# A vision tower with expert layer on one core: earlier queries and gather, constant products at the end, last quarter in two parts

## The chip, the core and the metric

One core of a Trainium2 chip runs the kernel. The metric is the device time of one execution in microseconds (us), the median of several runs. Engines: TensorE (PE; its weight loads are listed apart as PEld), VectorE (DVE), ScalarE (ACT), GpSimd (POOL) and SyncE (SP). Here POOL mostly issues indirect DMAs, and SP issues the plain ones.

## The reference

16 images of 128x512 become 1024 tokens of 64 numbers each. Everything is float32.

```
h = patches(x) @ W.T + b + pos                       # 8x8 patches
h = h + attention(layernorm(h))                      # 8 heads of 8; K softmax over tokens, Q softmax over channels,
                                                     # context = K V^T, out = Wr (context^T Q) + br, + its own input
z = layernorm(h)
p = softmax(z @ gate_w + gate_b); two best experts of 16, weights normed to sum 1
h = h + sum over the two: weight * ((silu(z @ w1[e]) * (z @ w2[e])) @ w3[e])
```

## The kernel before, in words

**Pairs and steps.** Images are taken two at a time, 8 pairs `m` = 0 to 7. All five engines have a program of their own, written out over one common count of steps `s` (the loops `for s in range(SPAN)`). A step is no barrier: it only fixes the order of an engine's instructions, and semaphores do the rest. Each pair has a plan, a tuple that gives for each of its attention and routing stages a time `k` within the pair; `step_of(m, k)` turns it into a step, mostly `BEGUN[m] + k`. Whole numbers, halves and three quarters are places in the step. On TensorE a step holds, in order: the expert layer's first product of group `g = s - 23` (`project_in`), `turn_hidden(g-1)`, the stages with whole `k` of the pairs under way (lower `m` first), `turn(g+2)`, `project_out(g-2)`, the stages at `k+0.5`, those at `k+0.75`, the turned gates, and the sums. VectorE and ScalarE have whole and half places only.

**Attention of a pair.** Embedding into `wide_ps` (L1407, L1413), its norm on DVE, a trip of the normed embedding through DRAM (`xi_scratch`, `hx`), keys (L1534) and their softmax, queries and values in four quarters `r` (`queries`, L1424 and L1427: one matmul of 512 columns for the biases and two of 256 columns; then DVE L1065 and L1068 take the maximum of each head and subtract it, ACT L784 copies the values), the exponential of the queries (ACT L787), the head sums (DVE L1035), context (PE L1460), scales (DVE L1074 to L1080), the mix (L1454), the turned queries (PE L1465, ACT L790), and the attention output (PE L1475, L1476). Quarters 0 and 2 share one half of `wide_ps`, 1 and 3 the other. Then the second norm, the gate's logits (L1481) and the choice of experts, `pick` (DVE L1135 to L1166, a chain of small operations), the rank of each token in its expert (PE L1545 to L1548, waiting for `hot_sum` of `pick`) and its place (`find_places`, DVE L1212 to L1255).

**Expert layer.** POOL scatters the normed rows of a pair to DRAM, sorted by expert (L682, 32 indirect DMAs of 128 rows: 16 columns x 2 experts); TensorE works through 98 groups of four tiles (12 a pair, 13 for pairs 6 and 7): turned rows (L1612), two matmuls per tile against the expert's first weights (L1634), turned hidden (L1650), second weights (L1658); each result `y` is stored to DRAM by SP (L486). POOL then gathers each pair's results with 32 indirect DMAs (L699), ACT weighs them (`weigh`, L873) and DVE adds (`sum_up`, L1343, L1347). `GATHER[m]` is the step at which pair `m`'s gather stands in POOL's program, `SUMS[m]` those of its sums. A gather first waits until the pair's `y` is all stored, and POOL's step waits for `turn` of group `s - 23 + 1`. Pair 6 and 7 are scattered in pieces of three rows (L669).

**The last pair.** Pair 7 is gathered in pieces, 16 indirect DMAs `gather_pieces` (L711), one for each of 16 columns (8 blocks of tokens x 2 images), right behind pair 6's gather in POOL's program. TensorE sums them with the gated routes (`sum_pieces`, L1602): three products of 96 rows by 128 by 64 columns per column of tokens, which the profile counts as two records each, so 24 records in a quarter of four columns. Each quarter waits for its four gathers, then DVE adds `h2` (`sum_up_pieces`, L1333), and SP stores two DMAs (`store_result`, L493). The last quarter stands at step 128. The quarters lie in `turn_ps`, `hidT_ps` and the two halves of `h_ps`.

**Products of constants.** `keep_on` (L1431 to L1434) multiplies the identity by `pos_in` (512 columns) into `turn_ps`, whose result nobody reads; it stands once in the program, six products in pair 2's step 4. The profile counts two records a product.

Of the kernel before, what the change touches and what calls it, by code (L numbers as in the profile page):

```python
# [15 lines left out]
P = 128  # L16
IMAGES, MELS, FRAMES = 16, 128, 512
PATCH = 8
E = 64
# [5 lines left out]
PAIRS = IMAGES // 2  # L25
# [46 lines left out]
AT_ONCE = FIRST._replace(zturn=12, logits=12.5, pick=12.5, rank=13, count=13, odds=14.5, base=13.5, ends=13.5, owner=14)  # L72
PLANS = (AT_ONCE._replace(mean=3.5), AT_ONCE._replace(mean=2.5, mixed=8.5), FIRST._replace(embed=(0.75, 0.75, 1.75, 2)),
         LATER, LATER, LATER, LATER._replace(rank=15.5, count=15.5, base=16, tiles=16, bases2=16.75, moves=17, ends=17.5, owner=18),
# [20 lines left out]
SUMS = ([[43 + 14 * m + q for q in range(4)] for m in range(4)]  # L95
        + [[94, 95, 96, 97], [107, 108, 109, 110], [122, 123, 123, 124], [125, 126, 127, 128]])
STORED = 2
QUARTERS = 4
WARM = 6

ALONG = {4: ("att_ps_ready", 6), 8: ("k_ps_ready", 3), 12: ("logits_ps_ready", 2)}
# [48 lines left out]
def vit_kernel(nc, x, tok_w, tok_b, pos, wk, bk, wq, bq, wv, bv, wr, br, gate_w, gate_b, w1, w2, w3, out):  # L150
# [4 lines left out]
    with ExitStack() as ctx:  # L155
# [210 lines left out]
        y_stored = [sem(f"y_stored{n}") for n in range(2)]  # L366
        gathered = [[sem(f"gathered{n}_{q}") for q in range(QUARTERS)] for n in range(2)]
        rows_zeroed = [sem(f"rows_zeroed{n}") for n in range(3)]
        block = ctx.enter_context(nc.Block())
# [12 lines left out]
        def sums_at(s):  # L382

            for m in range(PAIRS):
                for q in range(QUARTERS):
                    if s == SUMS[m][q]:
                        yield m, q
# [46 lines left out]

        def quarter_place(q):

            return (turn_ps[:, 0:COLS * E // QUARTERS], hidT_ps[:, 0:COLS * E // QUARTERS],
                    h_ps[:, 0:COLS * E // QUARTERS], h_ps[:, 512:512 + COLS * E // QUARTERS])[q]

# [5 lines left out]
        def _(sp):  # L445
# [42 lines left out]
            def store_result(m, q):  # L488
                wait(sp, "result_ready", QUARTERS * m + q + 1)
                for b in range(2):  # L490
                    t0 = q * BLOCKS // QUARTERS
                    dst = out[2 * m + b, t0 * P:(t0 + BLOCKS // QUARTERS) * P, :].rearrange("(t s) e -> s t e", s=P)
                    sp.dma_start(dst, result[apart(m)][:, t0:t0 + BLOCKS // QUARTERS, b, :]).then_inc(result_out[apart(m)], 16)  # L493

# [50 lines left out]
            for n, pairs in enumerate((PAIRS - 1, 1)):  # L545
                sp.wait_ge(result_out[n], 16 * 2 * QUARTERS * pairs)
            for n in range(3):
# [3 lines left out]
        def _(pool):  # L551
# [150 lines left out]
            def gather_pieces(m, j):  # L702

                q = j // (COLS // QUARTERS)
                if j == 0:
                    for n in range(2):
# [4 lines left out]
                gp.indirect_dma_start(y_pieces[j][0:PIECES, :], None, y_dram[m % 3].rearrange("(c i) e -> c (i e)", i=PIECE),  # L711
                                      bass.IndirectOffsetOnAxis(ap=piece_from[0:PIECES, j:j + 1], axis=0)).then_inc(gathered[0][q], 16)

# [197 lines left out]
        def _(dve):  # L911
# [416 lines left out]
            def sum_up_pieces(m, q):  # L1328
                blocks = slice(q * BLOCKS // QUARTERS, (q + 1) * BLOCKS // QUARTERS)
# [3 lines left out]
                ve.tensor_tensor(result[0][:, blocks], quarter_place(q).rearrange("p (t b e) -> p t b e", b=2, e=E), h2[m % RING][:, blocks],  # L1333
                                 ALU.add).then_inc(S["result_ready"], 1)
# [44 lines left out]
        def _(pe):  # L1379
# [50 lines left out]

            def keep_on():  # L1431

                for n in range(WARM):
                    te.matmul(turn_ps[:, :], ident[:, :], pos_in[:, :, :].rearrange("p t e -> p (t e)"), start=True, stop=True)  # L1434

            def attend(m, k):

                plan, wide_ps, side_ps = PLANS[m], wides[second(m)], sides[second(m)]
                if (m, k) == (2, X_NEXT):
                    keep_on()  # L1440
                for quarter in range(4):
# [149 lines left out]
            def sum_pieces(m, q):  # L1591

                if q == 0:
                    wait(pe, "gates_turned", COLS)
                    wait(pe, "rowsT_ready", GROUPS_ALL)
                    wait(pe, "hidT_ready", GROUPS_ALL)
                    wait(pe, "hid_done", 2 * GROUPS_ALL)
                wait_on(pe, gathered[0][q], 16 * 2 * COLS // QUARTERS * (gathers(m) - 1) + 16 * COLS // QUARTERS)
                for i in range(COLS // QUARTERS):
                    j = q * COLS // QUARTERS + i  # L1600
                    for n in range(PIECE):
                        mm = te.matmul(quarter_place(q)[:, i * E:(i + 1) * E], pieces[1][j][0:PIECES, n * P:(n + 1) * P],  # L1602
                                       y_pieces[j][0:PIECES, n * E:(n + 1) * E], start=(n == 0), stop=(n == PIECE - 1))
                mm.then_inc(S["y_ps_summed"], 1)
# [108 lines left out]
```

## Time and profile before

| | |
|---|---|
| median of 3 runs | 737.89 us (735.17 to 743.90) |
| the profiled execution's own time | 742.13 us |
| its span, first to last instruction | 740.4 us |
| mean granted TensorE clock | 0.906 of full speed |
| PE busy | 84% of the span |
| POOL busy | 66% |
| DVE busy | 67% |
| ACT busy | 49% |

A row of the timeline gives start, duration, engine, line, operation, output<-input, how many instructions were merged, and in brackets the idle time before and what ended it. A row of the chain gives start, duration and what the chain went through. A row of the windows gives busy time (and number of instructions) of PE, PEld, DVE, ACT and POOL in a stretch, then the granted clock of TensorE (1.00 is 2.4 GHz, 0.50 is 1.2 GHz), the DMA engines' share and GB/s.

### The profile page before, as it was taken

The page shows a single profiled execution, that of the slowest core. Times are in us where ns is not written, and L with a number is a line of the kernel's source. Part 1 is how long each engine was busy: PE and PEld are TensorE (multiplying, and loading weights), DVE is VectorE, ACT ScalarE, POOL GpSimd, SP SyncE. Part 2 cuts the span into 40 slices and gives each one's busy share as a digit, 9 for nine tenths or more (in the row PEclk, how much of TensorE's full clock was granted, in tenths as well). Part 3 has the DMA queues.
Part 4 walks back from the last instruction along what each step waited for, and adds up shares of the span by engine and source line. Part 5 has one row for each costly group of instructions (what it writes and reads, how often), then busy time and mean ns, then how long its engine had stood idle before and what let it go on. Part 6 is the DMA issues. An engine that isn't in the chain of part 4 may idle for free.

```text
span 740.4 us, 14231 instructions
## 1 busy us (share of the span) xinstructions
PE 619.8 (84%) x4126; PEld 517.0 (70%) x4126; DVE 493.4 (67%) x1369; ACT 361.4 (49%) x795; POOL 488.2 (66%) x521
## 2 busy tenths in 40 slices
PE   5886687679799998999979998997878877987938
PEld 3465455577589867886868687966768767977938
DVE  5654675667546776777667756768578797776920
ACT  2121323045355646664666456643656556766730
POOL 5354047767575677777777777777747756777773
PEclk9958899699899999999999989998889999988955
DMA  3398604244274347544745284536435446655442
GB/s 83 82 182 325 241 30 128 70 123 115 69 213 126 84 102 205 138 109 95 194 123 140 68 200 120 134 83 147 109 104 123 121 118 181 158 124 120 100 95 57
DMA packets 169740, 95.11 MB, mean 128 GB/s; under 512 B 99682, under 2 KB 153746, under 8 KB 169668
## 3 DMA queue, kind: packets, MB, share of 16 engines
q1 hardware_dynamic: 153524, 67.96, 36.1%
q0 software_dynamic: 15360, 25.85, 13.1%
q8 instruction: 39, 0.64, 0.4%
q10 hardware_dynamic: 784, 0.39, 0.2%
q14 instruction: 33, 0.27, 0.1%
HBM read 45.61 MB, written 48.55 MB: 127 GB/s over the span
## 4 chain that ended last, share of the span: by engine, by line
PE 52%; DVE 24%; issue 9%; DMA 6%; ACT 6%; POOL 2%; ACTq 0%; DVEq 0%; POOLq 0%
PE h_ps L1634 7%; PE wide_ps L1407 7%; PE y_ps L1658 6%; PE hidT_ps L1650 4%; PE turn_ps L1612 3%; PE wide_ps L1427 3%; DVE twice_y L1324 3%; DMA hx<-xi_scratch 3%; PE wide_ps L1534 2%; ACT sums L873 2%; DMA xi_scratch<-xi 2%; PE wide_ps L1413 2%; PE wide_ps L1475 1%; POOL sums L699 1%; PE wide_ps L1476 1%
## 5 line engine op out<-in xcount | busy, mean ns | idle before, releaser
L682 POOL DMA_INDIRECT rows_scratch<-z_parts,place x192 | 191.5, 998 | 106.4 <-issue 55.8
L699 POOL DMA_INDIRECT sums<-y_scratch,place x192 | 187.0, 974 | 66.2 <-issue 56.4
L1634 PE MATMUL h_ps<-w_hi,rowsT 128*128 (+1 forms) x392 | 116.3, 324 | 14.2 <-DVE hid_all L1326 14.1
L1324 DVE SCALAR_TENSOR_TENSOR twice_y<-tanh,h_ps 128x256 f32<-128x256 f32 (+1 forms) x196 | 81.1, 414 | 35.4 <-ACT tanh L826 22.3
L1634 PE MATMUL h_ps<-w_lo,rowsT 128*128 (+1 forms) x392 | 104.7, 293 | 0.0
L1658 PE MATMUL y_ps<-w_sb,hidT_all 128*128 (+1 forms) x784 | 101.9, 275 | 1.2 <-ACT twice_y L841 1.2
L1658 PEld LDWEIGHTS y_ps<-w_sb,hidT_all 128*128 128x128 f32 (+1 forms) x784 | 98.9, 198 | 1.6 <-issue 1.6
L1634 PEld LDWEIGHTS h_ps<-w_hi,rowsT 128*128 128x128 f32 (+1 forms) x392 | 78.0, 199 | 23.8 <-issue 20.2
L826 ACT ACTIVATE tanh<-h_ps 128x256 f32<-128x256 f32 (+1 forms) x196 | 70.3, 386 | 46.1 <-PE h_ps L1634 41.7
L1326 DVE SCALAR_TENSOR_TENSOR hid_all<-twice_y,h_ps 128x256 f32<-128x256 f32 (+1 forms) x196 | 82.4, 420 | 6.7
L1634 PEld LDWEIGHTS h_ps<-w_lo,rowsT 128*128 128x128 f32 (+1 forms) x392 | 78.7, 201 | 0.4
L1612 PE MATMUL turn_ps<-ident,rows_all 128*128 128x128 f32 (+1 forms) x392 | 62.8, 285 | 12.4 <-ACT rowsT L815 11.0
L1650 PE MATMUL hidT_ps<-ident,hid_all 128*128 128x128 f32 (+1 forms) x392 | 65.6, 294 | 6.1 <-issue 3.6
L815 ACT ACTIVATE rowsT<-turn_ps 128x512 fp32r<-128x512 f32 (+1 forms) x98 | 57.9, 591 | 25.6 <-PE turn_ps L1612 25.3
L835 ACT ACTIVATE hidT_all<-hidT_ps 128x512 f32<-128x512 f32 (+1 forms) x98 | 59.1, 603 | 15.1 <-PE hidT_ps L1650 13.6
L1612 PEld LDWEIGHTS turn_ps<-ident,rows_all 128*128 128x128 f32 (+1 forms) x392 | 47.5, 147 | 25.9 <-issue 23.5
L1407 PE MATMUL wide_ps<-w_patch,x_cols 64*128 64x512 f32 x224 | 56.1, 632 | 3.2 <-DVE w_patch L930 3.2
L1650 PEld LDWEIGHTS hidT_ps<-ident,hid_all 128*128 128x128 f32 (+1 forms) x392 | 47.3, 151 | 11.7 <-issue 11.1
L841 ACT ACTIVATE twice_y<-y_ps 128x256 f32<-128x256 f32 (+1 forms) x98 | 37.4, 381 | 12.0 <-PE y_ps L1658 7.3
L1343 DVE SCALAR_TENSOR_TENSOR sums<-sums,gate 128x64 f32<-128x64 f32 x96 | 20.9, 279 | 27.4 <-ACT sums L873 27.3
L784 ACT ACTIVATE vals<-wide_ps 128x256 f32<-128x256 f32 x28 | 10.8, 384 | 57.8 <-DVE qs L1068 57.8
L873 ACT ACTIVATE sums<-sums,mean_all,gate 128x64 f32<-128x64 f32 x96 | 34.2, 430 | 9.0 <-DMA sums<-y_scratch,place 9.0
(369 smaller groups left out, 1141.7 us busy)
## 6 DMA issues: line engine op xcount, KB each, us to landing
rows_all<-rows_scratch SPq DMA_DIRECT2D x72, 256.0 KB
rows_scratch<-tanh SPq DMA_DIRECT2D x3, 3276.0 KB
y_scratch<-twice_y SPq DMA_DIRECT2D x72, 128.0 KB
rows_all<-rows_scratch SPq DMA_DIRECT2D x26, 252.0 KB
xi_scratch<-xi SPq DMA_DIRECT2D x16, 256.0 KB
hx<-xi_scratch SPq DMA_DIRECT2D x14, 256.0 KB
out<-sums SPq DMA_DIRECT2D x56, 64.0 KB
x_in<-in_x SPq DMA_DIRECT2D x26, 128.0 KB
```

The costliest lines, as they stand in the source:

```text
L682: gp.indirect_dma_start(rows_dram[n], bass.IndirectOffsetOnAxis(ap=place[m % RING][:, r, j:j + 1], axis=0), z_parts[m % 2][:, j // 2, j % ...
L699: gp.indirect_dma_start(y_of[r][apart(m)][:, j // 2, j % 2, :], None, y_dram[m % 3][0:GROUPS[m] * GROUP * width(m), :], bass.IndirectOffse ...
L815: sc.activation(rowsT[g % 2][:, 0:GROUP * w], turn_ps[:, 0:GROUP * w], ACT.Copy).then_inc(S["rowsT_ready"], 1)
L826: sc.activation(tanh[0:w, j, :], h_ps[0:w, :].rearrange("p (j n h) -> p j n h", j=GROUP, n=2)[:, j, 0, :], ACT.Tanh, scale=0.5).then_inc(S ...
L835: sc.activation(hidT[g % 2][:, 0:GROUP * w], hidT_ps[:, 0:GROUP * w], ACT.Copy).then_inc(S["hidT_ready"], 1)
L1324: ve.scalar_tensor_tensor(twice[0:w, j, :], tanh[0:w, j, :], 1.0, halves[:, j, 0, :], ALU.add, ALU.mult).then_inc(S["twice_done"], 1)
L1326: ve.scalar_tensor_tensor(hid[g % 2][0:w, j, :], twice[0:w, j, :], 0.5, halves[:, j, 1, :], ALU.mult, ALU.mult).then_inc(S["hid_done"], 1)
L1407: te.matmul(wide_ps[:, b * 512:(b + 1) * 512], x_cols[second(m)][half, j, :], w_patch[half, j, :, :].rearrange("p t e -> p (t e)"), start= ...
L1612: mm = te.transpose(turn_ps[:, j * w:(j + 1) * w], rows[g % 3][0:w, j, :, :].rearrange("p n e -> p (n e)"), ident[0:w, 0:w])
L1634: mm = te.matmul(h_ps[0:w, j * 256:(j + 1) * 256], rowsT[g % 2][:, j * w:(j + 1) * w], w12[:, bass.ds(experts[g][j], 1), :, :].rearrange(" ...
L1650: mm = te.transpose(hidT_ps[:, j * w:(j + 1) * w], hid[g % 2][0:w, j, :], ident[0:w, 0:w])
L1658: mm = te.matmul(y_ps[0:w, j * E:(j + 1) * E], hidT[g % 2][:, j * w:(j + 1) * w], w3_sb[:, bass.ds(e, 1), :].rearrange("h a d -> h (a d)") ...
```

## The change

Four edits:

- Pair 2's plan: the four quarters of the queries stand at k = 5.75, 6, 6.5, 7 in place of 6, 6.5, 7, 7.5, their values (DVE and ACT) at 5.5, 6, 6.5, 7 in place of 6.5, 6.5, 7.5, 7.5, and the stages from the exponential to the mix half a step sooner. `attend`, the attention output, keeps k = 10.
- Pair 0's gather stands at step 37 of POOL's program in place of 38.
- Ahead of the last pair's sums TensorE runs products of constants into `side_ps`: four before the first part, two before the second, two before the third, one before the fourth, none before the fifth. The first ones wait for pair 6's last gather, for the last copied `y` and for the last owners.
- The last quarter is two parts of two columns each, with a semaphore of its own for the last two gathers (`gathered_last`), a place in `y_ps` for the fifth part, an addition on DVE for each part and two stores for each part.

```
-PLANS = (..., FIRST._replace(embed=(0.75, 0.75, 1.75, 2)),
+PLANS = (..., FIRST._replace(embed=(0.75, 0.75, 1.75, 2), queries=(5.75, 6, 6.5, 7), values=(5.5, 6, 6.5, 7), qexp=7, qsum=7.5, context=7.5,
+                             scales=8, mix=8, qturn=8.5, mixed=9),
-GATHER = (38, 51, 65, 78, 86, 99, 110, 123)
+GATHER = (37, 51, 65, 78, 86, 99, 110, 123)
-        + [..., [122, 123, 123, 124], [125, 126, 127, 128]])
+        + [..., [122, 123, 123, 124], [125, 126, 127, 128, 128]])
+PARTS = (0, 4, 8, 12, 14, 16)
+LATE = (4, 2, 2, 1, 0)
+        def part_signal(j):
+            return gathered_last if j >= PARTS[4] else gathered[0][j // (COLS // QUARTERS)]
+        def part_place(q):
+            return (turn_ps, hidT_ps, h_ps[:, 0:512], h_ps[:, 512:1024], y_ps)[q][:, 0:len(part_cols(q)) * E]
-            def keep_on():
-                for n in range(WARM):
-                    te.matmul(turn_ps[:, :], ident[:, :], pos_in[...], start=True, stop=True)
+            def keep_on(place, count):
+                for n in range(count):
+                    te.matmul(place[:, :], ident[:, :], pos_in[...], start=True, stop=True)
             def sum_pieces(m, q):
                 if q == 0:
                     ...
+                    wait(pe, "y_ready", GROUPS_ALL)
+                    wait(pe, "owner_ready", PAIRS)
+                    wait_on(pe, gathered[1][QUARTERS - 1], 16 * 2 * COLS // QUARTERS)
-                wait_on(pe, gathered[0][q], 16 * 2 * COLS // QUARTERS * (gathers(m) - 1) + 16 * COLS // QUARTERS)
-                for i in range(COLS // QUARTERS):
+                keep_on(side_ps, LATE[q])
+                if q < QUARTERS:
+                    wait_on(pe, gathered[0][q], 16 * 2 * COLS // QUARTERS * (gathers(m) - 1) + 16 * len(part_cols(q)))
+                else:
+                    wait_on(pe, gathered_last, 16 * len(part_cols(q)))
+                for i, j in enumerate(part_cols(q)):
                     ...
```

`store_result` and `sum_up_pieces` take the blocks of a part for the last pair, and the last wait of SP counts the two further stores.

## Rows read from the trace of the kernel before

**Rows 1.** The page's first part: busy time, share of the span, instructions

```profile
PE 619.8 (84%) x4126; PEld 517.0 (70%) x4126; DVE 493.4 (67%) x1369; ACT 361.4 (49%) x795; POOL 488.2 (66%) x521
```

**Rows 2.** The chain that ended last, its last pieces

```profile
713.79 2.68 DMA sums<-y_scratch,piece_from
...
716.61 5.35 PE turn_ps L1602 x24
...
727.08 10.25 PE h_ps L1602 x48
```

**Rows 3.** Windows of the end: idle stretch and the sums

```profile
707.00:716.50 9.50, 0.00 (x0) 0.00 (x0) 4.05 (x16) 3.32 (x10) 7.06 (x9) 0.50 0.50 111
716.60:737.40 20.80, 20.71 (x96) 20.53 (x96) 1.31 (x4) 0.00 (x0) 9.75 (x11) 0.50 0.25 62
```

**Rows 4.** Timeline of the end, and second products at the full clock

```profile
692.82 0.99 PE L1658 MATMUL y_ps<-w_sb,hidT_all 128*126 x8
...
711.23 1.43 ACT L873 ACTIVATE xi<-hx,mean_all,gate 128x64 f32<-128x64 f32 x4 [2.34 <-DMA kexp<-y_scratch,place]
...
728.48 0.91 POOL L711 DMA_INDIRECT sums<-y_scratch,piece_from  x1 [0.30 <-issue]
...
737.36 0.42 DVE L1333 TENSOR_TENSOR sums<-h_ps,h 128x256 f32<-128x256 f32 x1 [4.70 <-PE h_ps L1602]
```

**Rows 5.** Products of constants (timeline), keys (chain), and windows with the granted clock

```profile
112.37 5.31 PE L1434 MATMUL turn_ps<-pos_in,ident 128*128 128x512 f32 x12
...
39.07 3.78 PE wide_ps L1534 x4
...
43.00:49.00 6.00, 4.89 (x24) 4.49 (x23) 5.55 (x17) 2.31 (x4) 0.00 (x0) 0.50 1.23 182
...
112.40:117.70 5.30, 5.28 (x14) 2.06 (x12) 3.94 (x15) 2.03 (x3) 3.82 (x4) 1.00 0.70 183
143.30:146.70 3.40, 3.36 (x8) 2.72 (x9) 1.86 (x7) 0.49 (x2) 2.71 (x3) 0.50 0.25 69
146.70:151.00 4.30, 2.91 (x22) 2.48 (x22) 2.17 (x5) 1.71 (x3) 3.17 (x4) 1.00 0.74 224
```

**Rows 6.** Pair 2's queries and what follows: one window, then the timeline

```profile
131.90:135.10 3.20, 0.00 (x0) 0.00 (x0) 2.99 (x9) 0.00 (x0) 2.59 (x3) 0.50 0.13 41
...
137.12 0.77 PE L1424 MATMUL wide_ps<-qv_bias,ones_r 128*128 128x512 f32 x1
...
137.69 1.91 PE L1427 MATMUL wide_ps<-proj_qv,hx 128*128 128x256 f32 x4
...
142.00 0.41 DVE L1065 TENSOR_REDUCE qmax<-wide_ps 128x32 f32<-128x256 f32 x1
...
144.21 0.17 DVE L1170 TENSOR_SCALAR odds_sum<-odds 128x16 f32<-128x16 f32 x1 [0.56 <-ACT odds L809]
...
148.38 0.38 ACT L784 ACTIVATE vals<-wide_ps 128x256 f32<-128x256 f32 x1 [1.20 <-DVE qs L1068]
...
149.74 1.22 DVE L1035 TENSOR_REDUCE qsum<-qs 128x128 f32<-128x1024 f32 x1 [1.40 <-ACT qs L787]
...
153.37 1.09 PE L1465 MATMUL wide_ps<-ident,qs 128*128 128x128 f32 x8 [1.63 <-DVE qs L1080]
```

**Rows 7.** POOL: windows of two long stretches, and the timeline where it waited

```profile
244.00:540.00 296.00, 225.89 (x231) 0.96 0.52 129
...
628.20:729.40 101.20, 77.12 (x80) 0.84 0.50 118
...
155.18 0.96 POOL L682 DMA_INDIRECT rows_scratch<-z_parts,place  x1 [3.51 <-PE turn_ps L1612]
...
237.93 0.36 SPq L486 DMA_DIRECT2D y_scratch<-twice_y  x1
...
243.79 0.99 POOL L699 DMA_INDIRECT sums<-y_scratch,place  x1 [8.02 <-PE turn_ps L1612]
...
544.78 0.91 POOL L669 DMA_INDIRECT rows_scratch<-w_patch,piece_at  x1 [4.33 <-ACT w_patch L855]
```

More of the change, by code:

```diff
@@ L72 @@
 AT_ONCE = FIRST._replace(zturn=12, logits=12.5, pick=12.5, rank=13, count=13, odds=14.5, base=13.5, ends=13.5, owner=14)
-PLANS = (AT_ONCE._replace(mean=3.5), AT_ONCE._replace(mean=2.5, mixed=8.5), FIRST._replace(embed=(0.75, 0.75, 1.75, 2)),
+PLANS = (AT_ONCE._replace(mean=3.5), AT_ONCE._replace(mean=2.5, mixed=8.5), FIRST._replace(embed=(0.75, 0.75, 1.75, 2), queries=(5.75, 6, 6.5, 7), values=(5.5, 6, 6.5, 7), qexp=7, qsum=7.5, context=7.5,
+                                                                                               scales=8, mix=8, qturn=8.5, mixed=9),
          LATER, LATER, LATER, LATER._replace(rank=15.5, count=15.5, base=16, tiles=16, bases2=16.75, moves=17, ends=17.5, owner=18),
@@ L367, in vit_kernel @@
         gathered = [[sem(f"gathered{n}_{q}") for q in range(QUARTERS)] for n in range(2)]
+        gathered_last = sem("gathered_last")
         rows_zeroed = [sem(f"rows_zeroed{n}") for n in range(3)]
@@ L384, in sums_at @@
             for m in range(PAIRS):
-                for q in range(QUARTERS):
+                for q in range(len(SUMS[m])):
                     if s == SUMS[m][q]:
@@ L433, in piece_place, with part_cols, part_blocks @@
             return (turn_ps, hidT_ps)[j % 2][:, :] if in_between(m) else wide_ps[:, j % 2 * 512:(j % 2 + 1) * 512]
-        def quarter_place(q):
-            return (turn_ps[:, 0:COLS * E // QUARTERS], hidT_ps[:, 0:COLS * E // QUARTERS],
-                    h_ps[:, 0:COLS * E // QUARTERS], h_ps[:, 512:512 + COLS * E // QUARTERS])[q]
+        def part_cols(q):
+            return range(PARTS[q], PARTS[q + 1])
+        def part_blocks(q):
+            return slice(PARTS[q] // 2, PARTS[q + 1] // 2)
+        def part_signal(j):
+            return gathered_last if j >= PARTS[4] else gathered[0][j // (COLS // QUARTERS)]
+        def part_place(q):
+            return (turn_ps, hidT_ps, h_ps[:, 0:512], h_ps[:, 512:1024], y_ps)[q][:, 0:len(part_cols(q)) * E]
         def x_half(m, b, par):
@@ L490, in store_result @@
                 for b in range(2):
-                    t0 = q * BLOCKS // QUARTERS
-                    dst = out[2 * m + b, t0 * P:(t0 + BLOCKS // QUARTERS) * P, :].rearrange("(t s) e -> s t e", s=P)
-                    sp.dma_start(dst, result[apart(m)][:, t0:t0 + BLOCKS // QUARTERS, b, :]).then_inc(result_out[apart(m)], 16)
+                    blocks = part_blocks(q) if m == PAIRS - 1 else slice(q * BLOCKS // QUARTERS, (q + 1) * BLOCKS // QUARTERS)
+                    dst = out[2 * m + b, blocks.start * P:blocks.stop * P, :].rearrange("(t s) e -> s t e", s=P)
+                    sp.dma_start(dst, result[apart(m)][:, blocks, b, :]).then_inc(result_out[apart(m)], 16)
             def clear_rows(n):
@@ L545, in _ @@
             for n, pairs in enumerate((PAIRS - 1, 1)):
-                sp.wait_ge(result_out[n], 16 * 2 * QUARTERS * pairs)
+                sp.wait_ge(result_out[n], 16 * 2 * (QUARTERS * pairs + (len(PARTS) - 1 - QUARTERS) * (1 - n)))
             for n in range(3):
@@ L1328, in sum_up_pieces @@
             def sum_up_pieces(m, q):
-                blocks = slice(q * BLOCKS // QUARTERS, (q + 1) * BLOCKS // QUARTERS)
+                blocks = part_blocks(q)
                 wait(dve, "y_ps_summed", q + 1)
@@ L1429, in queries @@
                 mm.then_inc(S["qv_ps_ready"], 1)
-            def keep_on():
-                for n in range(WARM):
-                    te.matmul(turn_ps[:, :], ident[:, :], pos_in[:, :, :].rearrange("p t e -> p (t e)"), start=True, stop=True)
+            def keep_on(place, count):
+                for n in range(count):
+                    te.matmul(place[:, :], ident[:, :], pos_in[:, :, :].rearrange("p t e -> p (t e)"), start=True, stop=True)
             def attend(m, k):
@@ L1439, in attend @@
                 if (m, k) == (2, X_NEXT):
-                    keep_on()
+                    keep_on(turn_ps, WARM)
                 for quarter in range(4):
@@ L1597, in sum_pieces @@
                     wait(pe, "hid_done", 2 * GROUPS_ALL)
-                wait_on(pe, gathered[0][q], 16 * 2 * COLS // QUARTERS * (gathers(m) - 1) + 16 * COLS // QUARTERS)
-                for i in range(COLS // QUARTERS):
-                    j = q * COLS // QUARTERS + i
+                    wait(pe, "y_ready", GROUPS_ALL)
[7 more added lines that the diff above has]
+                for i, j in enumerate(part_cols(q)):
                     for n in range(PIECE):
-                        mm = te.matmul(quarter_place(q)[:, i * E:(i + 1) * E], pieces[1][j][0:PIECES, n * P:(n + 1) * P],
+                        mm = te.matmul(part_place(q)[:, i * E:(i + 1) * E], pieces[1][j][0:PIECES, n * P:(n + 1) * P],
                                        y_pieces[j][0:PIECES, n * E:(n + 1) * E], start=(n == 0), stop=(n == PIECE - 1))
```

7 lines of the change are left out of this document (3 added, 4 removed).

## The prediction, made before the changed kernel was run

> **What bounds the kernel now.** I read the page's busy shares, then the chain that ended last, then windows of its end, then POOL's timeline. The shares name no single engine: PE is busy 84% of the span, DVE 67%, POOL 66% [rows 1]. But POOL's busy time leaves out 0.30 us between two indirect DMAs. From 244 to 540 it issued 231 in 296 us, 1.28 us each, and from 628.2 to 729.4 80 in 101.2 us, 1.265 us each [rows 7]: there it never stops. In between it waits for others, as 4.33 us for a piece that ACT had to copy [rows 7]. So the first 628 us go at the pace of TensorE with DVE and ACT; from there POOL's 80 gathers (two pairs of 32 and 16 pieces) set the time, whatever TensorE does, until the last lands.
>
> The end is a second matter. The chain ends with a gather that takes 2.68 us to land, then 24, 24 and 48 records of L1602, 20.7 us in one piece [rows 2]. TensorE stood idle from 707 to 716.5 with its clock at 0.50 (1.2 GHz), and the clock stayed at 0.50 through all 96 records of the sums, 20.71 us busy of 20.80 [rows 3]. A record takes 10.25 / 48 = 0.213 us, a quarter 5.12 us. POOL supplies a quarter in 4.90 us: from the fourth gather at 713.79 [rows 2] to the sixteenth at 728.48 [rows 4] are twelve of 1.224. So TensorE at half clock is just slower than the supply, falls behind a little in each quarter, and starts the last one late: the last gather starts at 728.48, lands 2.7 us later at 731.2, and the last addition comes at 737.36 [rows 4], 6.2 us behind.
>
> **The change part by part.**
>
> *Products and the fifth part.* At the full clock the nearest rows to the sums are the second products (the same loads, 64 columns streamed): 8 records in 0.99 us, 0.124 each with the tail of the last one in it [rows 4]; half of 0.213 is 0.107. I take 0.112. So a full quarter takes 24 x 0.112 = 2.7 us and a half one 12 x 0.112 = 1.34 us. A product of constants took 5.31 / 6 = 0.88 us at clock 1.00 [rows 5]; at 0.50 I take the keys, of the same 512 columns, two matmuls in 3.78 us, 1.89 us each [rows 5].
>
> The first four products may start when pair 6's last gather has landed, 711.2 by ACT's wait for it [rows 4]. All four at 0.50 would end at 718.8. If the clock comes back after 3.4 us of them, as it did in the queries [rows 5], 1.8 are done and the other 2.2 take 1.9 us: 716.5; some us later or sooner moves this end by half as much. I take 717. The first four gathers of pieces are in at 716.5 [rows 2], so the others at 721.4, 726.3, 728.7 and 731.2. With the clock back, TensorE does this: part 1 from about 717 to 719.7, two products to 721.5, part 2 (in at 721.4) to 724.2, two products to 726.0, part 3 (in at 726.3) to 729.0, one product to 729.9, part 4 (in at 728.7) to 731.2, part 5 (in at 731.2) to 732.6. Each product lies in time in which TensorE would wait for POOL; no gap is above 0.6 us. The addition starts at 732.7 in place of 737.36: 4.65 us gained. Its cost falls from 0.42 to some 0.25 us, while two more stores go through SP, about 0.4 us each beside the last gathers; I count these as nothing together (-0.2 to +0.8). The new waits of TensorE hold nobody up: behind them stand only the sums, which could not start before 716.5. The range of this term: if the clock comes back during the sums, 2 to 4.6 us gained; if it never does, a loss (the rival below). I take 4.65, because products of constants kept the clock at 1.00 over 5.3 us, and because after 3.4 us of queries at 0.50 (8 records, 256 and 512 columns) it was at 1.00 again [rows 5]; ours are up to 7.6 us of the longest kind.
>
> One row speaks against this: the keys, 3.78 us without a pause at 0.50, were followed by six more microseconds at 0.50 [rows 5]. Twice that length lies before the first part, and the pairs of products between the parts come on top.
>
> The sums' own row says that their kind of work does not raise the clock: 20.7 us busy, and 0.50 to the last [rows 3]. The Trainium skill (TensorE: Matmul & The Clock Gate, Part 1: The HAM clock gate) says that the throttle is the default and that sustained activity of the engine releases it. By that rule the sums of before would have freed themselves in the first quarter, and the products would only take up time. This trace does not agree, at 0.213 us per record from the first to the last.
>
> *Queries of pair 2.* TensorE stood idle from 131.9 to 135.1, waiting for pair 1's `pick` on DVE [rows 6]. Quarter 0 of the queries costs 2.48 us at half clock (137.12 to 139.60) [rows 6]; at k = 5.75 it is ahead of pair 1's rank and fits into that hole. Its DVE part follows `pick` at 135.2 and is done by 136.1. Then, with the durations of rows 6: rank to 137.1 as before, quarter 1 to 139.6, its DVE part to 140.6, pair 1's `find_places` behind it to 142.7 (0.6 later than before), quarters 2 and 3 on TensorE meanwhile (to 143.4), their DVE parts of 0.9 us each to 144.5, the last copy of values to 144.9. Before, it ended at 148.76: 3.85 gained. A part is given back: pair 1's odds stand on ACT behind the exponential of pair 2 now, and DVE must do its weights (the four operations from 144.21 on [rows 6], some 0.2 each) before the head sums. These start at 147.1 in place of 149.74 [rows 6], 2.6 gained. The scales follow, so the turned queries come at 150.8 in place of 153.37 [rows 6], and so do the attention output and group 0. POOL, which waited 3.51 us for `turn` of group 1 at 155.18 [rows 7], starts 2.6 sooner. Bounds: 0 if one of the waits stays where it is, 3.85 if the weights cost nothing. I take 2.6.
>
> From there to 628 us nothing waits for a fixed time: all orders are as before, so the shift is carried by every engine. That is the weak step, over 470 us.
>
> *Pair 0's gather.* It started at 243.79, released by `turn` at step 38 [rows 7]. At step 37 the wait is for the last `y`, issued at 237.93 [rows 7] and in about 2.2 us later: a start at 240.5 or so, 3.3 sooner. Since POOL runs without a pause from there to 540, it keeps these 3.3 us, and then they go into the wait of 4.33 us for a piece at 544.78 [rows 7]: it becomes some 7.6. Nothing on TensorE waits long for these gathers or scatters before. I take 0; bounds: -0.5 (traffic met at another time) to 3.3 (all of it kept).
>
> **Sum.** 742.13 - 4.65 - 2.6 - 0 = 734.9 for the profiled execution. It lies 4.24 above the median shown, 737.89; the same 7.25 off the median gives 730.6.
>
> **Rivals.**
> A. *The clock does not come back at the end.* Then every product costs 1.89 us on the path: 711.2 + 4 x 1.89 = 718.8, first part to 723.9, 3.78 more, 5.12, 3.78, 5.12, 1.89, and 5.12 for parts 4 and 5: 748.7 in place of 737.3, 11.4 lost, less 2.6 from the front: 746.7. For it: the keys and the sums at 0.50. Against it: the queries and the products before. It decides from the point where the clock is still 0.50 at the end of part 2. Slower.
> B. *The front's gain is used up on the way* (a hole in TensorE's program, as DVE's chains leave, simply gets longer). Then only the end counts: 737.89 - 4.65 = 733.2. For it: POOL's and TensorE's many waits between 540 and 628. Against it: nothing there depends on time that the change does not move too.
> C. *The lead of POOL counts too*, because rows or stores wait for its scatters somewhere: up to 3.3 more, 727.3. For it: POOL has no pause in 296 us. Against it: the wait at 544.78, where POOL is the one that waits.
> D. *The clock comes, and falls again in the sums*, whose kind of work did not raise it: then one or two parts run at 0.213 us a record and 2 to 4 us of the 4.65 are lost: 733.6.
>
> **How the numbers follow.** The forecast 0.50, A 0.07, B 0.19, C 0.10, D 0.10; 0.04 is left for what I don't see. A measurement of this kernel can tell about 1% from no change, here 7.4 us, and the forecast, 730.6, lies on that bound of 730.5. Faster by over 1%: half of the forecast's chance, all of C, and some of the rest: 0.42. Within 1%: the other half, B and D: 0.51. Slower by over 1%: A: 0.07. The range goes from C (727) to above B and D with the runs' own spread: 736.
>
> **What would show it.** Right: TensorE's windows from about 716 on at 1.00, sum records 0.112 us apart, 64 columns as before; gaps of TensorE below 1 us between parts; the last addition some 1.5 us behind the landing of the last gather, at about 730 in the trace's time; quarter 0 of pair 2's queries in the hole near 132; head sums near 147.1; POOL's wait before pair 1's second lot of scatters below 1 us; POOL's last saturated run starting at 625.6. Wrong: any 0.50 window in the sums; head sums later than 148.5; a saturated run that starts at 628 or later.

## The result, and the profile after

| | before | changed |
|---|---|---|
| median of 20 runs each, taken side by side | 741.14 us (734.80 to 746.66) | 735.29 us (732.09 to 739.82) |
| the profiled execution's own time | 742.13 us | 738.46 us |
| its span | 740.4 us | 736.7 us |

The ratio is 0.9938, with a 95% interval of 0.9919 to 0.9957: the changed kernel is 0.6% faster (the two medians alone divide to 0.9921, near the lower end of that interval). Six of the study's 268 executions are recorded as slow (more than 1.5% above the fastest of their kernel) and left out of the ratios and of the fit below. The ratio's gain is 0.4% of the time less than the forecast (730.6 / 737.89 = 0.990). The 737.89 it started from was a low draw of three runs; over 117 runs of the kernel before, in all comparisons of this study, the mean is 740.6. In the changed kernel's profile the full level of TensorE's clock reads 0.95 where it reads 1.00 in the one before (the half level reads 0.50 in both). Of TensorE's times at the full level only the wide products are longer for it; rows for this stand at the experiment with the gather's step taken back.

The page's busy line and the last pieces of its chain (columns as in [rows 1, 2]):

```profile
PE 627.2 (85%) x4144; PEld 513.3 (70%) x4144; DVE 493.0 (67%) x1370; ACT 361.4 (49%) x795; POOL 488.1 (66%) x521
```

```profile
706.35 2.54 DMA kexp<-y_scratch,place
709.03 6.65 PE side_ps L1450 x8
715.68 2.64 PE turn_ps L1624 x24
718.32 1.84 PE side_ps L1450 x4
720.16 2.65 PE hidT_ps L1624 x24
722.80 1.85 PE side_ps L1450 x4
724.66 2.64 PE h_ps L1624 x24
...
728.25 1.29 PE h_ps L1624 x12
729.54 1.36 PE y_ps L1624 x12
```

The busy shares are those of [rows 1]; only PE's rose, by 7.4 us. Products were added and sums shortened, but the traces of this study with the same number of PE records spread from 619.4 to 629.5 us, so no cause is read from these 7.4 us. The chain shows the end that I forecast: four products in 6.65 us, mostly at half clock, then every full part in 2.64 us, where the first took 5.35 and the last two together 10.25 before [rows 2]. Windows of the same stretch (columns as in [rows 3]):

```profile
709.10:715.60 6.50, 6.50 (x10) 2.70 (x10) 1.30 (x5) 1.25 (x4) 4.98 (x6) 0.54 0.37 89
715.70:731.10 15.40, 15.19 (x106) 12.50 (x105) 1.74 (x5) 0.00 (x0) 8.65 (x10) 0.95 0.32 80
```

Granted clock 0.54 during the products and the full level in all five parts, where [rows 3] had 0.50 throughout. The timeline has POOL's last gather and the last addition:

```profile
726.18 0.91 POOL L727 DMA_INDIRECT sums<-y_scratch,piece_from  x1 [0.30 <-issue]
...
730.93 0.29 DVE L1349 TENSOR_TENSOR sums<-y_ps,h 128x128 f32<-128x128 f32 x1 [1.06 <-PE y_ps L1624]
```

The last addition starts 4.75 us behind the last gather's start; before it was 737.36 - 728.48 = 8.88 [rows 4]. So 4.13 us were gained at the addition, and yet the span ends 736.7 - 726.18 = 10.5 us behind the last gather, where before it ended 11.9 behind: 1.4 us gained. What lies between stands in the instructions that the trace puts on the program's block itself (here L155 before and L160 after; the columns are engine, operation, count, duration in ns min/median/max, first and last start). Before:

```profile
L155 POOLq DRAIN  x1: 22113/22113/22113, 716.7 to 716.7; - x1
...
L155 SPq DRAIN  x1: 7/7/7, 740.2 to 740.2; - x1
```

After:

```profile
L160 POOLq EVENT_SEMAPHORE  x2: 17/17/17, 736.5 to 736.6; - x2
...
L160 POOLq DRAIN  x1: 22273/22273/22273, 714.2 to 714.2; - x1
...
L160 SPq DRAIN  x1: 7/7/7, 733.3 to 733.3; - x1
```

A DRAIN stands at the end of each engine's program, with only semaphore events behind it. POOL's is recorded from early on, while its gathers are still being worked off, so its start says little; what matters is its end, start plus duration: 716.7 + 22.1 = 738.8 before and 714.2 + 22.3 = 736.5 after. Both are 10.30 us behind the start of the last gather. SyncE, which waits for the last result stores, reached its own DRAIN at 740.2 before and at 733.3 after. Before, the stores ended the run and POOL's drain was through 1.4 us earlier; after, the stores are done at 733.3 and the run waits for POOL to 736.5. The chain does not show this: it follows work, and ended with TensorE's last part.

The front in the timeline of after, first TensorE and VectorE around pair 2's queries, then POOL:

```profile
129.39 0.77 PE L1440 MATMUL wide_ps<-qv_bias,ones_r 128*128 128x512 f32 x1
...
132.15 0.61 DVE L1181 TENSOR_REDUCE hot_sum<-hot_b 128x16 f32<-128x256 bf16 x1
...
132.82 0.21 PE L1561 MATMUL hidT_ps<-ones,hot_sum 128*16 128x1 f32 x2 [0.95 <-DVE hot_sum L1181]
...
144.72 0.17 DVE L1186 TENSOR_SCALAR odds_sum<-odds 128x16 f32<-128x16 f32 x1 [1.50 <-ACT odds L825]
...
145.43 1.20 DVE L1051 TENSOR_REDUCE qsum<-qs 128x128 f32<-128x1024 f32 x1
```

```profile
150.85 0.95 POOL L699 DMA_INDIRECT rows_scratch<-z_parts,place  x1 [1.07 <-PE turn_ps L1634]
...
238.00 0.99 POOL L716 DMA_INDIRECT sums<-y_scratch,place  x1 [6.58 <-DMA y_scratch<-twice_y]
...
542.13 0.91 POOL L686 DMA_INDIRECT rows_scratch<-w_patch,piece_at  x1 [4.66 <-ACT w_patch L871]
...
625.88 0.97 POOL L716 DMA_INDIRECT sums<-y_scratch,place  x1 [0.30 <-issue]
```

Quarter 0 lies in the hole, whose rest is 0.95 us where it was 3.2 [rows 6]. Odds and weights now stand ahead of the head sums, which start at 145.43, 4.3 us sooner than the 149.74 of [rows 6]; but 2.3 of these were there already at pair 1's `hot_sum` (132.15 against 134.46, from other stretches at half clock ahead of it), so the queries' own share is 2.0. POOL's wait at 155.18 of 3.51 [rows 7] is one of 1.07, pair 0's gather starts at 238.00, released by the stored `y` and no longer by `turn`, and the unbroken run of 80 starts at 625.88 for 628.20: 2.3 us sooner. That this is near the 2.6 forecast is luck: head sums that start 4.3 us sooner should have moved it by 4.3, and from `hot_sum` to the last gather both traces take 594.0 us.

### The profile page after: what moved, and what is told of

The parts are those of the page before. It is cut to its first block, busy times and chain, and to the rows that moved or that the text cites. A ratio compares the mean times of both kernels' runs of the same rounds, so it can differ in the third digit from the quotient of the medians.

```text
span 736.7 us, 14271 instructions
## 1 busy us (share of the span) xinstructions
PE 627.2 (85%) x4144; PEld 513.3 (70%) x4144; DVE 493.0 (67%) x1370; ACT 361.4 (49%) x795; POOL 488.1 (66%) x521
## 4 chain that ended last, share of the span: by engine, by line
PE 51%; DVE 24%; issue 9%; ACT 6%; POOL 5%; DMA 4%; ACTq 0%; DVEq 0%; POOLq 0%
PE wide_ps L1423 7%; PE h_ps L1656 7%; PE y_ps L1680 5%; PE hidT_ps L1672 3%; PE turn_ps L1634 3%; PE wide_ps L1443 3%; DVE twice_y L1340 2%; PE wide_ps L1550 2%; POOL sums L716 2%; ACT sums L889 2%; PE wide_ps L1429 2%; DMA hx<-xi_scratch 2%; PE side_ps L1450 2%; DMA xi_scratch<-xi 1%; PE wide_ps L1491 1%
## 5 line engine op out<-in xcount | busy, mean ns | idle before, releaser
L1656 PE MATMUL h_ps<-w_hi,rowsT 128*128 (+1 forms) x392 | 116.5, 325 | 14.1 <-DVE hid_all L1342 13.9
L1656 PEld LDWEIGHTS h_ps<-w_hi,rowsT 128*128 128x128 f32 (+1 forms) x392 | 78.5, 200 | 24.4 <-issue 20.7
L1672 PEld LDWEIGHTS hidT_ps<-ident,hid_all 128*128 128x128 f32 (+1 forms) x392 | 46.1, 148 | 11.1 <-issue 10.3
L1423 PEld LDWEIGHTS wide_ps<-w_patch,x_cols 64*128 64x128 f32 x224 | 21.2, 194 | 24.2 <-issue 19.7
```

What stands on the lines that cost most here:

```text
L1423: te.matmul(wide_ps[:, b * 512:(b + 1) * 512], x_cols[second(m)][half, j, :], w_patch[half, j, :, :].rearrange("p t e -> p (t e)"), start= ...
L1656: mm = te.matmul(h_ps[0:w, j * 256:(j + 1) * 256], rowsT[g % 2][:, j * w:(j + 1) * w], w12[:, bass.ds(experts[g][j], 1), :, :].rearrange(" ...
L1672: mm = te.transpose(hidT_ps[:, j * w:(j + 1) * w], hid[g % 2][0:w, j, :], ident[0:w, 0:w])
```

## The experiments

Two theories after the result. The drain theory (called D in the expectations below; it is not the prediction's rival D): the front's gain arrived, and at the end only 1.4 us counts, because POOL's drain, 10.3 us behind its last gather, takes over from the stores. Its rival (E, with the prediction's B): the end was gained in full as computed, and most of the front's 2.6 us was lost on the way. A third question is which of the two front edits carries the front. All ratios are against runs of the kernel before on the same chip.

**One group of edits each.** The plan of pair 2 and the gather's step, with the old end:

```
-PLANS = (..., FIRST._replace(embed=(0.75, 0.75, 1.75, 2)),
+PLANS = (..., FIRST._replace(embed=(0.75, 0.75, 1.75, 2), queries=(5.75, 6, 6.5, 7), ...),
-GATHER = (38, ...
+GATHER = (37, ...
```

> Only the first two edits (pair 2's plan, pair 0's gather at step 37); the end is as before. Theory D (the end is held by POOL's drain, which ends 10.3 us after the start of the last gather, so the products and parts gain only about 1.4 us and the front carries the rest): 3 to 4 us below before, ratio 0.995 to 0.996; POOL's last run without a pause starts 2 to 4 us sooner than 628.2. Rival E (the end's 4.6 us are all gained and the front's are used up on the way, as rival B of the prediction said): within 1 us of before, ratio 0.999 to 1.001.

Measured: 736.96 us, ratio 0.9948 (0.9920 to 0.9976). In its trace the last 80 gathers start at 621.15, 7.1 us sooner than before, where 2 to 4 were expected: single executions differ by more than the edits are worth.

The products and the fifth part, with the old plan and step:

```
+LATE = (4, 2, 2, 1, 0)
+PARTS = (0, 4, 8, 12, 14, 16)
```

> Only the products and the fifth part; the front is as before. Theory D: 1.4 us below before, ratio 0.998; in the trace the last addition about 4.7 us after the start of the last gather, SyncE through some 7.2 us after it, POOL's drain 10.3 us after it, and the span ends 0.2 us behind that. Rival E: 4 to 5 us below before, ratio 0.994, and the end follows the last addition by about 3 us.

Measured: 738.64 us, ratio 0.9987 (0.9957 to 1.0017). The front carries the larger part and the end at most 0.43%, where the prediction gave it 4.65 us (0.63%). The two ratios multiplied give 0.9935, within the changed kernel's interval. E falls: its 0.994 for the end alone and its 0.999 to 1.001 for the front alone both lie outside the intervals. The trace of this kernel adds a case that the prediction had as its own rival D, the clock falling again in the sums (TensorE's timeline):

```profile
722.91 1.55 PE L1623 MATMUL h_ps<-sums,w_patch 96*128 96x64 f32 x12 [0.21 <-DMA sums<-y_scratch,piece_from]
724.30 1.50 PE L1623 MATMUL h_ps<-sums,x_in 96*128 96x64 f32 x12
725.64 1.96 PE L1449 MATMUL side_ps<-pos_in,ident 128*128 128x512 f32 x2
727.39 2.66 PE L1623 MATMUL h_ps<-sums,x_cols 96*128 96x64 f32 x12
729.84 2.77 PE L1623 MATMUL y_ps<-sums,squares 96*128 96x64 f32 x12
```

The last product takes 1.96 us and both half parts 2.7 instead of 1.5; the last addition comes 7.4 us behind the last gather (732.65 - 725.24). The span ends 10.5 us behind it all the same, by the drain. What I priced at 2 to 4 us in rival D costs nothing here.

**No products.** The changed kernel with

```
-LATE = (4, 2, 2, 1, 0)
+LATE = (0, 0, 0, 0, 0)
```

> The changed kernel without any product of constants (a count of 0 for each part); parts, waits and front stay. Sums run at clock 0.50 to the end, 0.213 us a record, the last addition about 8.9 us after the last gather's start. Theory D: the store of the last part then ends after POOL's drain again, so 1.0 to 1.5 us above the changed kernel, ratio to before about 0.996. Rival E: 4 to 5 us above the changed kernel, ratio to before 0.999 to 1.000.

Measured: 736.19 us, ratio 0.9925 (0.9897 to 0.9953), not to be told from the changed kernel; the 0.996 that the drain theory gave lies just outside, and E's 0.999 to 1.000 far outside. In its trace the last addition is 8.8 us behind the last gather and the span ends 11.4 behind it, by the stores, 0.9 later than with products. So by the trace all products together are worth 0.9 us, not four; the ratio, with an interval of 0.56%, cannot show so little.

**The drain itself.** The changed kernel with a wait on POOL for the landing of the last two gathers, and a no-operation behind it:

```
+                if j == COLS - 1:
+                    pool.wait_ge(gathered_last, 32)
+                    gp.nop()
```

> The changed kernel, with one wait more on POOL behind the last gather: for the landing of the last two gathers, then a no-operation. It asks what POOL's drain waits for. If it is a cost of its own that starts when POOL's last instruction is through, its end moves by the landing, 2.5 us and more, to 12 to 13 us after the last gather's start. If it is work left from the indirect DMAs themselves, it ends 10.3 us after the last gather's start as before, and the time stays.

Measured: 735.96 us in its one run, span 734.2. POOL's last gather starts at 721.93 in the timeline, and the block's instructions read:

```profile
L160 POOLq EVENT_SEMAPHORE  x2: 17/17/17, 734.0 to 734.1; - x2
...
L160 POOLq DRAIN  x1: 9381/9381/9381, 724.6 to 724.6; - x1
```

Now the DRAIN starts only when the gathers have landed, and its own length shows: 9.38 us. It ends 724.6 + 9.4 = 734.0, 12.03 us behind the last gather instead of 10.30, and the span follows it. So the 9.4 us are a cost of their own that begins when POOL is through with its last instruction (10.30 less the 0.91 of the gather is 9.39), not the landing of a transfer: a drain that only waited for the landing would have been over at once. This rests on one execution, but on its trace and not on its time.

**The two front edits apart.** The plan alone, and the step alone:

```
-PLANS = (..., FIRST._replace(embed=(0.75, 0.75, 1.75, 2)),
+PLANS = (..., FIRST._replace(embed=(0.75, 0.75, 1.75, 2), queries=(5.75, 6, 6.5, 7), ...),
```

> The kernel before with the new plan of pair 2 alone; the gather stays at step 38 and the tail is the old one. If the front's gain is the queries' (my prediction's 2.6 us, carried to the end): POOL's last run of 80 starts about 2.6 us sooner and the median is about 2.6 us (0.35%) below the kernel before, ratio 0.9965, nearly all of what both front edits together gave (0.9948). If instead POOL's lead carried the gain: no measurable difference, ratio 1.000. The end stays 11.9 us behind the last gather's start, by SyncE's stores.

Measured: 738.79 us, ratio 0.9986 (0.9951 to 1.0022).

```
-GATHER = (38, ...
+GATHER = (37, ...
```

> The kernel before with pair 0's gather at step 37 alone. If, as predicted, POOL's lead is swallowed by its wait for ACT's copied piece near 544 us: the gather starts 3 to 4 us sooner (about 240), the wait near 544 grows by as much, ratio 1.000 (-0.07% to +0.1%). If the lead counts at the end (rival C): up to 3.3 us faster, ratio 0.9955 to 0.997, and the run of 80 starts sooner than 628.2 by as much.

Measured: 741.12 us, ratio 0.9983 (0.9945 to 1.0021). Neither can be told from no change alone, and each interval holds both expectations. The trace of the plan alone, of the fastest of its 12 executions, has the last 80 gathers at 619.19, 9 us sooner, far from the 2.6 expected and again more than the edit. POOL's timeline of the second shows the mechanism:

```profile
238.61 0.99 POOL L699 DMA_INDIRECT sums<-y_scratch,place  x1 [4.93 <-DMA y_scratch<-twice_y]
...
544.77 0.91 POOL L669 DMA_INDIRECT rows_scratch<-w_patch,piece_at  x1 [6.19 <-ACT w_patch L855]
...
628.18 0.97 POOL L699 DMA_INDIRECT sums<-y_scratch,place  x1 [0.30 <-issue]
```

The gather starts 5.2 us sooner than the 243.79 of [rows 7] (1.8 of that were there at `hot_sum`), the wait near 544 grows from 4.33 to 6.19, another of 2.19 us stands at 537.67 where before there was none of over 2 us, and the last run starts at 628.18 against 628.20. In this execution the lead is gone by then, as the prediction had it. So is the lead of the head sums, which start at 145.57 here, 4.2 us sooner than before. Over all traces the growth of the waits is clearer: POOL's pauses of over 0.4 us between 300 and 560 us sum to 8.2 us on average in the four traces with step 38 and to 11.8 in the ten with step 37.

**Undone one at a time.** With the intervals so wide, the same question from the other side, the changed kernel with one front edit taken back:

```
-GATHER = (37, ...
+GATHER = (38, ...
```

> The changed kernel with pair 0's gather back at step 38. By my prediction (worth 0): the same as the changed kernel, ratio to the kernel before 0.994. By a least-squares fit over all runs so far, in which the step is worth 1.2 us with an uncertainty of 0.6: ratio 0.9955. By rival C (3.3 us): 0.9985.

Measured: 737.84 us, ratio 0.9956 (0.9921 to 0.9990). The interval holds all three expectations, that of the prediction's C too. The chain of this trace, whose full level reads 1.00, has two products and a full part:

```profile
717.88 1.77 PE side_ps L1450 x4
719.65 2.63 PE hidT_ps L1624 x24
```

In the changed kernel's chain, at 0.95, they took 1.84 and 2.64 us: the products are 4% longer and the sums are not.

```
-PLANS = (..., FIRST._replace(embed=(0.75, 0.75, 1.75, 2), queries=(5.75, 6, 6.5, 7), ...),
+PLANS = (..., FIRST._replace(embed=(0.75, 0.75, 1.75, 2)),
```

> The changed kernel with the old plan of pair 2; gather at 37 and the new tail stay. If the queries carry 2.0 to 2.6 us: ratio to the kernel before 0.9965 to 0.9975 (738.3 to 738.9). If they carry nothing to the end (rival B): 0.994, as the changed kernel. The local step shows in the stretch from pair 1's pick to group 0: about 20 us with the old plan, 17 to 18 with the new.

Measured: 737.69 us, ratio 0.9993 (0.9965 to 1.0021). By this ratio, taking the plan back gives up nearly all of the gain; median by median (737.69 / 739.84 = 0.9971) it gives up about half, as in the fit below, and as the 0.9965 to 0.9975 expected. The 0.994 that the prediction's B would give lies outside the interval. In its trace the head sums start 13.65 us behind `hot_sum`, and the last addition 4.15 behind the last gather, with the clock at its full level throughout the parts.

One kernel's runs spread over 1%, so I put them into one least-squares fit: 262 runs of 14 kernels, a level for each of the four groups of comparisons, a yes or no for each edit (kernels that differ from the changed one in their products or POOL's last wait count as having the new end), and one for the three kernels at the end of this section.

| edit | forecast, us | fitted, us, with 95% interval |
|---|---|---|
| pair 2's plan | -2.6 | -2.1 +/- 0.9 |
| pair 0's gather at 37 | 0 | -1.05 +/- 0.93 |
| products and five parts | -4.65 | -1.1 +/- 1.0 |
| the three together | -7.25 | -4.2 +/- 0.9 |

**Products ahead of the first part alone.** The changed kernel with

```
-LATE = (4, 2, 2, 1, 0)
+LATE = (4, 0, 0, 0, 0)
```

> The changed kernel with the four products ahead of the first part alone, and none between the later parts. If they raise the clock by themselves: the first part's 24 records take 2.65 us. If the products between keep it up: a later part falls to 0.50 (5.1 us for a full part, 2.6 for a half), and the last addition comes up to 4 us later behind the last gather. Either way the end stays 10.5 us behind the last gather, by POOL's drain, and the ratio to the kernel before is that of the changed kernel, 0.994, since even a last addition 7.4 us behind the gather leaves SyncE before the drain's end. If the sums bound the end: 1 to 3 us slower than the changed kernel.

Measured: 737.33 us, ratio 0.9962 (0.9930 to 0.9994). Its TensorE timeline:

```profile
713.70 2.79 PE L1624 MATMUL turn_ps<-sums,w_patch 96*128 96x64 f32 x24
717.95 4.26 PE L1624 MATMUL hidT_ps<-sums,w_patch 96*128 96x64 f32 x24 [1.46 <-DMA sums<-y_scratch,piece_from]
722.79 2.82 PE L1624 MATMUL h_ps<-sums,w_patch 96*128 96x64 f32 x12 [0.57 <-DMA sums<-y_scratch,piece_from]
725.40 2.77 PE L1624 MATMUL h_ps<-sums,x_in 96*128 96x64 f32 x12
...
730.52 2.77 PE L1624 MATMUL y_ps<-sums,squares 96*128 96x64 f32 x12
```

Part 1 runs at the full clock, and in part 2, after 1.46 us of waiting, the clock falls and stays down: 2.8 us for twelve records from then on. So here the four products raise it and do not keep it up. That those between the parts do is borne out by six of the eight traces that have them; in the other two the clock fell all the same, but only in the last product. The last addition is 8.16 us behind the last gather, and the span ends 10.80 behind: here the stores (10.58) are barely behind the drain (10.30), where the expectation had the drain at the end. The median is 2 us above the changed kernel's, where the trace's own difference is 0.3; the intervals overlap, so it does not contradict.

**Looking for a better version.** If the end is POOL's unbroken run plus its drain, gathers must leave that run. Pair 5's gather one step sooner puts four of them among pair 7's scatters, where POOL has gaps:

```
-GATHER = (37, 51, 65, 78, 86, 99, ...
+GATHER = (37, 51, 65, 78, 86, 98, ...
```

> The changed kernel with pair 5's gather one step sooner in POOL's program (98 in place of 99). If from some 626 us on the time is that of POOL's unbroken run of gathers and of its drain 10.3 us behind the last one, then gathers that go into POOL's idle gaps of 0.5 to 4.3 us among pair 7's scatters shorten the run: some 2 to 4 fewer than 80 in the last unbroken run, last gather 2 us or so sooner, median about 2 us (0.27%) below the changed kernel, ratio to the kernel before about 0.991. If TensorE or the stores of the last group bound the end instead, nothing is gained (0.9938) or, where the earlier gathers wait for a store still under way, up to 1.5 us are lost.

Measured: 734.93 us, ratio 0.9927 (0.9888 to 0.9966), which holds the 0.991 expected and the changed kernel's 0.9938 alike.

Two steps sooner puts eight there:

```
-GATHER = (37, 51, 65, 78, 86, 99, ...
+GATHER = (37, 51, 65, 78, 86, 97, ...
```

> The changed kernel with pair 5's gather two steps sooner in POOL's program (97 in place of 99). One step moved four gathers ahead of the last scatters (last unbroken run 628.7 to the end, 76 gathers) and the time was 0.9927 of the kernel before, against 0.9938. If POOL's remaining gaps among pair 7's scatters (2.9, 1.2, 1.8, 0.5, 1.8 and 0.8 us) can take gathers, the second step brings a further 1 to 2 us: ratio 0.990 to 0.992. If those gathers must wait for the last y of pair 5 or push the scatters that TensorE's next groups wait for, the gain is gone: 0.994 or more.

Measured: 734.78 us, ratio 0.9917 (0.9886 to 0.9949). POOL's timeline of the second, among the scatters:

```profile
611.44 0.91 POOL L686 DMA_INDIRECT rows_scratch<-w_patch,piece_at  x1 [0.30 <-issue]
612.66 0.97 POOL L716 DMA_INDIRECT sums<-y_scratch,place  x1 [0.30 <-issue]
...
617.69 0.93 POOL L686 DMA_INDIRECT rows_scratch<-w_patch,piece_at  x1 [0.30 <-issue]
```

The gaps behind 611 are gone: POOL's pauses of over 0.4 us between 560 and 640 us sum to 6.3 us, against 9.6 to 11.0 in the eleven traces with this gather at 99. The ratio's interval holds the expected 0.990 to 0.992 and the changed kernel's 0.9938. The last has the gather at 98, and pair 1's odds and weights behind pair 2's head sums:

```
-         AT_ONCE._replace(mean=2.5, mixed=8.5)
+         AT_ONCE._replace(mean=2.5, mixed=8.5, odds=15.5)
```

> The changed kernel with pair 5's gather at 98 and pair 1's odds one step later (15.5), behind pair 2's head sums. The weights' four small operations on DVE, about 0.7 us, and the wait for ACT's odds leave the path between pair 2's exponential and its head sums: group 0 comes 0.7 to 1 us sooner against pick, and the time is 0.7 to 1 us below that of the kernel with gather at 98 alone, ratio 0.991 to 0.992. If something else then binds the head sums (the exponential itself, as at the old place), no difference: 0.9927.

Measured: 736.70 us, ratio 0.9960 (0.9929 to 0.9991). Locally it does what was expected: DVE's row before the head sums is no longer a weight but an idle stretch that waits for the exponential,

```profile
145.65 1.22 DVE L1051 TENSOR_REDUCE qsum<-qs 128x128 f32<-128x1024 f32 x1 [1.29 <-ACT qs L803]
```

11.05 us behind `hot_sum` (134.60) against 12.14 in the kernel with 98 alone. The total does not show it: both expected ratios, 0.991 to 0.992 and 0.9927, lie below the interval. The three together fit to -0.8 +/- 1.2 us against the changed kernel. With a term for each they fit to -1.4 +/- 1.9 (98), -2.1 +/- 1.8 (97) and +0.9 +/- 1.8 (odds later): 97 is the best candidate, but as the best of three and just off zero it isn't shown to beat the changed kernel.

## Why the prediction was right or wrong

*The size of the gain.* Forecast 7.25 us for the profiled execution; measured 742.13 - 738.46 = 3.67, and -4.2 +/- 0.9 over all runs. The direction was right; 735.29 us lies inside the range of 727 to 736, but nearly all of the missing part belongs to one term.

*The step that failed: "The addition starts at 732.7 in place of 737.36: 4.65 us gained."* The sentence takes the last addition for the end of the span. The addition did come that much sooner: 4.13 us at a full level that reads 0.95, and 4.7 in the trace of the kernel with the old plan (last addition 4.15 behind the last gather; 4.2 was forecast). But a second thing ends behind the last gather, POOL's drain at +10.30, and it was only 1.6 us below the end of before at +11.90. The term is capped there: 11.90 - 10.53 = 1.37 us, fitted 1.1. With the cap in place of 4.65 the forecast for the profiled execution would have been 742.13 - 1.37 - 2.6 = 738.2; it was 738.46. That this is so close is luck, since a single execution varies by more; what bears the cap out is the fit and the table. The DRAIN's row stood in the trace of before, outside the chain and the timeline of work. A table of the traces shows the rule (us behind the start of the last gather):

| trace | last addition | stores in (SyncE) | POOL's drain ends | span ends |
|---|---|---|---|---|
| before | 8.88 | 11.68 | 10.30 | 11.90 |
| plan and gather | 8.87 | 11.67 | 10.30 | 11.89 |
| no products | 8.79 | 11.21 | 10.30 | 11.43 |
| four products | 8.16 | 10.58 | 10.30 | 10.80 |
| end alone | 7.41 | 9.82 | 10.31 | 10.54 |
| changed | 4.75 | 7.17 | 10.30 | 10.53 |
| wait on POOL | 4.10 | 6.51 | 12.03 | 12.27 |

In each row the span ends 0.22 to 0.24 behind the later of the two middle columns. The seven other traces follow the same rule: 10.53 in the five with all products, 11.84 and 11.86 in the two with the old end, POOL's drain at 10.30 in all seven.

*The clock (forecast 0.50, A 0.07, D 0.10).* Right in every trace with products ahead of the first part: it came back before the first part and A never occurred. It fell again within the last product in two traces (the end alone, and gathers at 97) and stayed in the six others with all products, so the prediction's D is real, and costless under the drain. The Trainium skill (TensorE: Matmul & The Clock Gate, Part 1: The HAM clock gate) has sustained activity release the throttle. The runs bear out what the prediction held against it: the sums alone, 64 columns a record, never raised the clock in the kernel before [rows 3], and with four products they ran to the end at half clock once it had fallen; products of 512 columns raised it each time.

*The queries (-2.6).* Right in mechanism, a little large. In the traces with the old plan the head sums start 15.28, 13.67, 12.95 and 13.65 us behind pair 1's `hot_sum` (mean 13.9); in the nine with the new plan and the odds where they were 12.2 on average: 1.7 us. At the end 2.1 +/- 0.9. The step I called weak, that the shift is carried over 470 us, held on average, by the fit: from `hot_sum` to the last gather the four traces with the old plan take 594.0 us and the seven with the new one (pair 5's gather at 99) 590.8, 3.3 +/- 2.7 us less. No single trace shows it: between the traces of before and after this stretch is the same, and with the gather's step alone the head sums' lead of 4.2 us is gone at 628.

*Pair 0's gather (0).* The lead goes into POOL's waits, as I said: 3.6 us more of pauses between 300 and 560 us with step 37, for 3.3 computed, though not in one wait (in the changed kernel's trace the one near 542 is 4.66 us, and 6.22 with the step taken back). The fit gives -1.05 +/- 0.93, just off zero. Between nothing and 2 us is what I can say; the 3.3 us of C are excluded by the fit. Through what a microsecond would arrive is not shown.

*The chances.* They do not add up as written: half of the forecast's 0.50 and C's 0.10 make 0.35 for faster by over 1%, and the other half with B and D 0.54 for within 1%; with the 0.04 left over, 0.42 and 0.51 cannot be reached. The result, 0.6% faster, lies within 1%.

*The weakest number I left out:* the spread of single executions. The stretches at half clock fall differently each time, and the time ahead of pair 1's `hot_sum` alone, ahead of which the edits change nothing on VectorE, varied from 131.2 to 135.1 us between traces. A shift of 2 us of a single execution is below that. The 4.24 us between the profiled execution and the median of three were such noise: against the median of 20, 741.14, they are 1.0.

## What to carry to other kernels

Before an edit at the end of a program is given a price, list everything that must be over before the span ends, the drains of each engine included, and cap the gain at the distance to the second-latest; a chain of work does not list them. With indirect DMAs on GpSimd to the end, that engine's drain, not the last result, may be the floor, as it was here: then take work out of its last unbroken run. Products that nobody reads can hold the clock for narrow matmuls, but are worth only the time until the next thing that must be over: here 0.9 us of some 4.

## What the runs showed of the hardware

- POOL's DRAIN behind its last indirect DMA takes 9.4 us (10.30 behind the start of the last gather in all traces without the extra wait, to 0.01), and it is not the landing of the transfers: 9.38 us with a wait for the landing ahead of it. What it does in that time stays open; whether it is shorter behind other work on POOL wasn't tried.
- The full level of the granted clock read 0.95 in one execution, the changed kernel's profile, and 1.00 in all others; a full part of the sums took 2.64 us there and 2.63 at 1.00, two products of 512 columns 1.84 and 1.77.
- The sums do not raise the clock: 20.7 us of them ran at half clock [rows 3], and with four products alone it fell within the part behind a wait of 1.46 us and did not come back in the 13 us to the end. With products between the parts too it fell in two of eight traces, within the last product.
